# Key scale from raw keys, key splits inside the head steps, and the first score row through two banks

## The reference

```python
x = x + xattn(layernorm(x), ctx_512, ...)      # 16 heads over 4096 context rows of width 128
x = x + attn(layernorm(x), ...)                # 16 heads over the 256 tokens
x = x + ffn(layernorm(x), ...)                 # quantised weights and activations

# xattn, the part that this change touches
q_big = rope((hidden_q @ Wq.T per head) @ w_kc_q)        # 384 per head
kv_r  = rope(kv_c)                                       # 4096 x 128
scores = (q_big @ W_qr) . (kv_r @ W_kr)
attn  = softmax(scores)
ctx   = (attn @ kv_r) @ w_kc_kv
out   = ctx @ Wo.T
```

## Time and profile before

| | before |
|---|---|
| median of 3 runs | 576.0 us (575.85 to 577.02) |
| the profiled execution | 576.91 us, span 575.0 us |
| mean granted TensorE clock | 0.979 |
| TensorE, VectorE, ScalarE, GpSimd busy | 92%, 84%, 63%, 27% of the span |
| share of TensorE in the chain that ended last | 63% |

### The profile page before, as it was taken

One profiled execution on the slowest core, in us unless ns is written; L12 is line 12 of the kernel. 1 busy time (PEld: TensorE's weight loads), 2 busy tenths in 40 slices (PEclk: granted clock), 3 DMA queues, 4 the chain that ended last, 5 costly groups with the idle time before them and its releaser, 6 DMA issues.

```text
span 575.0 us, 9999 instructions
## 1 busy us (share of the span) xinstructions
PE 530.1 (92%) x3799; PEld 352.6 (61%) x3803; DVE 482.6 (84%) x716; ACT 363.4 (63%) x442; POOL 153.4 (27%) x186
## 2 busy tenths in 40 slices
PE   7999955789999999999999999999989998996896
PEld 3876722356666666666666666666667773454442
DVE  3588796899989999999999999999977366489986
ACT  1133460978788688687786886887885334896142
POOL 2359943101112202202102102201000001598401
PEclk9999996999999999999999999999998998999799
DMA  8998127599999999999999999999999989100001
GB/s 315 338 364 255 63 49 174 159 203 196 201 193 204 200 190 204 210 212 210 206 199 205 203 196 203 197 201 205 196 194 181 273 358 395 82 0 1 1 0 38
DMA packets 287806, 107.41 MB, mean 187 GB/s; under 512 B 276896, under 2 KB 277920, under 8 KB 286368
## 3 DMA queue, kind: packets, MB, share of 16 engines
q1 hardware_dynamic: 287776, 107.01, 85.6%
HBM read 37.26 MB, written 0.52 MB: 66 GB/s over the span
## 4 chain that ended last, share of the span: by engine, by line
PE 63%; DVE 18%; DMA 5%; issue 5%; ACT 4%; POOL 4%; SPq 0%; DVEq 0%; ACTq 0%
PE ps L646 16%; PE ps L648 8%; PE ps L628 8%; PE ps L630 8%; PE ps L629 8%; DMA pT<-split 4%; PE ps L748 4%; DVE rows L1233 3%; POOL qrope L480 2%; DVE split L1215 2%; DVE qrope L1265 2%; DVE qrot L1271 1%; DVE KL L1253 1%; PE ps L677 1%; PE ps L850 1%
## 5 line engine op out<-in xcount | busy, mean ns | idle before, releaser
L646 PE MATMUL ps<-pT,VH 128*128 128x256 f16 x1024 | 196.8, 274 | 1.9 <-DMA pT<-split 1.9
L648 PE MATMUL ps<-pT,VL 128*128 128x128 f16 x1024 | 183.4, 220 | 0.0
L1233 DVE TENSOR_SCALAR_CACHE_REDUCE rows<-ps,qback 128x1024 f32<-128x1024 f32 x128 | 163.6, 1280 | 17.5 <-PE ps L630 16.8
L1003 ACT ACTIVATE split<-rows,rz 128x2048 f16<-128x2048 f32 x64 | 124.8, 1995 | 67.5 <-DVE rz L1184 67.4
L1215 DVE SCALAR_TENSOR_TENSOR split<-rows,rz,split 128x2048 f16<-128x2048 f32 x64 | 150.3, 2350 | 1.3 <-issue 1.2
L989 ACT ACTIVATE rows<-rows,negm 128x2048 f32<-128x2048 f32 x64 | 127.2, 1988 | 0.2 <-DVE negm L1238 0.2
L646 PEld LDWEIGHTS ps<-pT,VH 128*128 128x128 f16 x1024 | 100.5, 98 | 42.8 <-DMA pT<-split 4.9
L648 PEld LDWEIGHTS ps<-pT,VL 128*128 128x128 f16 x1024 | 100.6, 98 | 27.3
L628 PE MATMUL ps<-KH,qcur 128*128 128x512 f16 x256 | 97.8, 382 | 14.0 <-DVE qcur L1290 10.7
L509 POOL TENSOR_TENSOR ctx_c<-acc 128x128 f32<-128x128 f32 x32 | 24.4, 762 | 296.8 <-ACT acc L978 296.8
L629 PE MATMUL ps<-KL,qcur 128*128 128x512 f16 x256 | 97.5, 381 | 0.0
(11 more groups left out here) (172 smaller groups left out, 656.1 us busy)
## 6 DMA issues: line engine op xcount, KB each, us to landing
w_sb<-w SPq DMA_DIRECT2D x3, 2816.0 KB, 15.8
wq_sb<-wq SPq DMA_DIRECT2D x4, 1024.0 KB, 8.6
wo_sb<-wo SPq DMA_DIRECT2D x16, 256.0 KB, 4.5
wkcq_sb<-wkcq SPq DMA_DIRECT2D x4, 768.0 KB, 9.3
keys<-ctxT SPq DMA_DIRECT2D x8, 256.0 KB, 7.7
stage<-ctxT SPq DMA_DIRECT2D x16, 128.0 KB, 8.0
stage<-kcos SPq DMA_DIRECT2D x8, 256.0 KB, 7.8
stage<-ksin SPq DMA_DIRECT2D x8, 256.0 KB, 9.3
```

Of the source, the lines that this page charges most:

```text
L646: nc.tensor.matmul(bank(6 + r % 2, 0, 256), VH[:, 4 * b + k, :], p.rearrange("p x q -> p (x q)"), start=(b == 0 and k == 0), stop=False)
L648: last = nc.tensor.matmul(bank(6 + r % 2, 0, 128), VL[:, 4 * b + k, :], p[:, 0, :], start=False, stop=(b == 7 and k == 3))
L1003: nc.scalar.activation(split[:, split_slot(r, half), :, 0, :], rows[:, k, half * 2048:(half + 1) * 2048].rearrange("p (b k) -> p b k", k=1 ...
L1233: nc.vector.tensor_scalar(rows[:, k, c * 1024:(c + 1) * 1024], ps[:, score_bank(s) * 512:(score_bank(s) + 2) * 512], qback[:, r // 2:r // ...
```

## The change

On SyncE, the raw load of a block of keys leaves `load_ctx` and becomes `load_raw`, with a semaphore of its own, and most raw loads are moved ahead of others. On ScalarE, the magnitude sums are taken of the raw keys, as soon as they are loaded, in place of the rotated ones. A rotated pair (a, b) mixes the two partitions 64 apart, so VectorE adds to each sum that of the other half (`kother`). The key scale is then made at p = 8 in place of 14; the products of the keys (GpSimd) come in other steps and wait for the magnitude sum of their block; KH and KL are made block by block in steps 9 to 13 and 10 to 14 in place of 15 to 17 and 16 to 18. The first query total moves from 16 to 10, the first query's halves from 18 to 15. Row 0's score steps come two by two at the end of steps 15 to 18, all through banks 0 and 1, with their copies in VectorE's steps 16 to 19; four steps of row 1 come at the start of steps 19 and 20. The key transposes wait for all rotated keys in place of all projections.

The sum of magnitudes before the rotation is not that after it, so the scale has another value than before; it is divided out again later.

```diff
-    EARLY = NCH
-    KEY_STEP = (0, 3, 5, 7, 8, 10, 11, 12)
-    HIGH_FIRST = (0, 3, 6, NCH)
-    LOW_FIRST = (0, 2, 4, NCH)
+    EARLY, EARLY_COPIED = NCH + 4, NCH + 2
+    RAW_STEP = (-1, 2, 4, 4, 5, 5, 6, 6)
+    KEY_STEP = (0, 2, 4, 6, 8, 9, 10, 11)
+    HIGH_STEP = (9, 9, 9, 10, 10, 11, 12, 13)
+    LOW_STEP = (10, 10, 10, 11, 11, 12, 13, 14)
...
+            def load_raw(n):
+                blk = slice(n * 512, (n + 1) * 512)
+                sp.dma_start(keys[:, blk], ctxT[:, blk]).then_inc(raw_in[n], 16)
...
             load_wq(0)
+            load_raw(0)
             load_ctx(0)
...
+            load_raw(1)
             load_ctx(1)
             load_wq(1)
+            load_raw(2)
+            load_raw(3)
             load_wqr(0)
...
+            load_raw(4)
+            load_raw(5)
+            load_ctx(2)
             load_wq(2)
-            load_ctx(2)
+            load_raw(6)
+            load_raw(7)
             load_wkcq(1)
             load_ctx(3)
...
-            sp.wait_ge(qhk_done, XH // 2)
+            sp.wait_ge(kr_done, NCH)
...
-                    pool.wait_ge(ctx_in[n % 4], 80 * (n // 4 + 1))
+                    pool.wait_ge(kabs_done, n + 1)
+                    pool.wait_ge(ctx_in[n % 4], 64 * (n // 4 + 1))
...
                     if j % 2 == 0:
-                        wait(pe, row_copied, 4 * row + j // 2 - 2)
-                    o = bank(score_bank(s) + j % 2)
+                        wait(pe, row_copied, j // 2 if first_row else 4 * row + j // 2 - 2)
+                    o = bank((0 if first_row else score_bank(s)) + j % 2)
...
+                if 19 <= p < 21:
+                    for s in range(2):
+                        attention_step(0, TURN - 8 + 2 * (p - 19) + s)
...
-                if p == 16:
+                if p == 10:
                     query_total(0)
-                if p >= 18:
-                    first = TURN - 16 + (0, 4, 6, 8)[p - 18]
-                    for s in range(first, TURN - 16 + (4, 6, 8, 8)[p - 18]):
-                        attention_step(0, s)
+                if 15 <= p < 19:
+                    for s in range(2):
+                        attention_step(0, TURN - 16 + 2 * (p - 15) + s)
...
+            def raw_sum(n):
+                act.wait_ge(raw_in[n], 16)
+                wait(act, kabs_done, n)
+                key = slice(n * 512, (n + 1) * 512)
+                nc.scalar.activation(absolute[:, :], keys[:, key], ACT.Abs, accum_out=kpart[:, n:n + 1]).then_inc(kabs_done, 1)
...
-                if 15 <= p < 18:
-                    for n in range(HIGH_FIRST[p - 15], HIGH_FIRST[p - 14]):
+                for n in range(NCH):
+                    if HIGH_STEP[n] == p:
                         key_high(n)
-                if p == 18:
+                if p == 15:
                     act.wait_ge(qhk_done, XH // 2)
...
+                for a, b in ((0, 64), (64, 0)):
+                    link(nc.vector.tensor_copy(kother[a:a + 64], ksum[b:b + 64]))
+                link(nc.vector.tensor_tensor(ksum[:, :], ksum[:, :], kother[:, :], ALU.add))
...
-                if p == 14:
+                if p == 8:
                     key_scale()
-                if p == 15:
+                if p == 9:
                     query_part(0)
-                if p == 17:
+                if p == 11:
                     query_factor(0)
...
-                if 16 <= p < 19:
-                    for n in range(LOW_FIRST[p - 16], LOW_FIRST[p - 15]):
+                for n in range(NCH):
+                    if LOW_STEP[n] == p:
                         key_low(n)
-                if p == 18:
+                if p == 15:
                     dve.wait_ge(qcur_first, 1)
...
+                if 16 <= p < 21:
+                    attention_step(0, 33 + 2 * (p - 16))
...
-            attention_step(0, 33)
-            attention_step(0, 35)
-            attention_step(0, 37)
-            attention_step(0, 39)
             query_part(1)
             query_factor(1)
-            attention_loop(dve, attention_step, EARLY, AVLAG)
+            attention_loop(dve, attention_step, EARLY_COPIED, AVLAG)
```

More of the change, by code:

```diff
@@ L164, in program @@
         ksum = small("ksum", [128, 1])
+        kother = small("kother", [128, 1])
         kinv = small("kinv", [128, 1])
@@ L298, in program @@
         ctx_in = [sem(f"ctx_in{k}") for k in range(4)]
+        raw_in = [sem(f"raw_in{k}") for k in range(NCH)]
         wo_in = [sem(f"wo_in{k}") for k in range(4)]
@@ L944, in _ @@
                     nc.scalar.activation(qrT[:, n // 2 % 2, :], bank(6, 0, TOK), ACT.Copy).then_inc(qr_copied, 1)
-                if p - 2 in KEY_STEP:
-                    n = KEY_STEP.index(p - 2)
-                    act.wait_ge(kr_done, n + 1)
-                    wait(act, kabs_done, n)
-                    key = slice(n * 512, (n + 1) * 512)
-                    nc.scalar.activation(absolute[:, :], keys[:, key], ACT.Abs, accum_out=kpart[:, n:n + 1])\
-                        .then_inc(kabs_done, 1)
-                if 15 <= p < 18:
-                    for n in range(HIGH_FIRST[p - 15], HIGH_FIRST[p - 14]):
+                for n in range(1, NCH):
+                    if RAW_STEP[n] == p:
+                        raw_sum(n)
+                for n in range(NCH):
+                    if HIGH_STEP[n] == p:
                         key_high(n)
-                if p == 18:
+                if p == 15:
                     act.wait_ge(qhk_done, XH // 2)
@@ L1231, in attention_step @@
                             dve.wait_ge(qbig_done, XH)
+                    o = 0 if isinstance(i, int) and row == 0 else score_bank(s)
                     nc.vector.tensor_scalar(rows[:, k, c * 1024:(c + 1) * 1024],
[L1234 removed]
+                                            ps[:, o * 512:(o + 2) * 512], qback[:, r // 2:r // 2 + 1], None,
                                             ALU.mult, ALU.max, accum_out=mx[:, k, c:c + 1]).then_inc(row_copied, 1)
```

10 lines of the change are left out of this document (4 added, 6 removed).

## The result

| | before | after |
|---|---|---|
| median | 575.9 us (575.84 to 577.02, 4 runs) | 595.0 us (592.98 to 595.96, 4 runs) |
| the profiled execution, its span | 576.91, 575.0 | 594.23, 592.0 |
| mean granted TensorE clock of it | 0.979 | 0.971 |
| end of the first query | 92.54 | 90.27 |
| first exponential | 103.23 | 119.66 |

A forecast was written before the change was run, and what follows sets the result against it. TensorE bounds the kernel (92% busy), so a shift of the first rows moves the end one for one. First query -4.4 and two-bank scores +14.2 give +9.8, taken as +9.0 on 576.0: 585.0 us, range 579.5 to 590.

The forecast's parts named there:

- the closed chain: Steps 16 and 17: scores, head product, signal, rotation and copy wait for each other in turn, 6.7 us each, 13.4 together.
- paper: Each engine's queue through the head laid out by hand in program order, with VectorE and GpSimd operations excluding each other.
- gain at the first query: End of the head: key splits taken out of TensorE's gap make the first query ready 4.4 us earlier.
- query to exponential, waits: First query to first exponential: row 0 through two banks takes 24.9 us against 10.7, 14.2 lost.
- deduction for the layout's lateness: First exponential: +9.8 taken as +9.0, because the old order's layout runs late where GpSimd and VectorE collide.
- rival (b): Steps 15 to 18: TensorE's clock falls to half, some 5 us of its work doubles: 590 us, chance 0.11.
- The layout of the old order: Hand-laid queues of the kernel before: first query at 94.2 (trace 92.54), first exponential at 104.7 (trace 103.23).
- the sum of loads: Head: raw blocks 3 to 7 ahead of the second key-query weights, which come 3.6 us later, at 35.8.
- (a): Steps 10 to 14: low halves hardly wait for GpSimd, 0.61 each, +4.9: 581 us, chance 0.15.
- (c): Head: VectorE keeps up, the gap is gone, TensorE's work hides the copies; 6 us faster, 570, chance 0.07.
- (d): Head: no collisions, query at 77.4, but the closed chain; exponential at 102.3, 575 us, chance 0.05.
- (e): Head: the change fails its purpose, for instance high halves wait for a late scale; slower still, chance 0.02.

The follow-up runs named there:

- experiment 6: The changed kernel with the second group of key-query weights loaded ahead of raw blocks 4 to 7: 593.4 us, ratio 1.029.
- experiment 1: The changed kernel with matmuls nobody reads put into TensorE's waits in the head, to keep its clock up: 589.3 us, ratio 1.022.
- experiment 3: The changed kernel with low halves subtracting a PSUM bank in place of KH (one SBUF input, result not the real one): 581.6 us, ratio 1.008.
- experiment 4: The changed kernel with row 0's scores put back to steps 18 to 20 and four banks, copies after the loop: 577.8 us, ratio 1.001.
- experiment 5: The kernel of experiment 4, but with row 0's scores through banks 0 and 1 alone: 581.9 us, ratio 1.007.
- experiment 9: The kernel of experiment 4 with key products earlier, low halves over steps 10 to 16 reading high halves from PSUM, first query in 16: 574.6 us, ratio 0.995.
- experiment 7: The kernel before the change with 39 matmuls nobody reads in its 10.67 us gap before row 0's first score: 576.1 us, ratio 0.996.
- experiments 9 and 11: The latter: the kernel of experiment 9 with matmuls nobody reads before the first query total and row 0's first score: 573.2 us, ratio 0.994.
- experiment 10: The changed kernel with VectorE's score copies ahead of rotations in steps 16 to 20, and unread matmuls in steps 10, 13, 15: 585.0 us, ratio 1.014.

## Why the prediction was wrong, step by step

**What held.** The direction; the closed chain, found before the run by reading two queues side by side, at 6.8 us a pair against 6.7; step 14 at 71.96 (paper 72.7); the first query at 90.27 (paper 89.8); the low halves at over 2 us beside GpSimd; the wait for weights in step 6 at 2.19, where 2 to 3 were forecast, harmless (experiment 6); the wait at the first total, 1.82 against 2.3; VectorE's steps 8 to 13, 35.3 us together against 36.2; the shift carried on nearly one for one.

**The sum at the first exponential: 9.0 forecast, 16.4 measured.** The 7.4 between them:

| step of the sum | forecast | measured | missed |
|---|---|---|---|
| gain at the first query | -4.4 | -2.3 | 2.1 |
| query to exponential, waits | +14.2 | +14.9 | 0.7 |
| query to exponential, clock | 0 | +3.8 | 3.8 |
| deduction for the layout's lateness | -0.8 | 0 | 0.8 |
| sum | +9.0 | +16.4 | 7.4 |

The measured 14.9 is 18.7 less 3.8 of experiment 1.

**The step that failed most** is the clock. It stood as rival (b) with 0.11, though its size was well found (some 5 us, measured 3.8 by this part and 5.7 by the medians). The argument against it was that the stretch that fell was busy for 3.40 of 8 us and that the new one would be busy for about half of its time. After had 5.67, 4.60 and 4.61 busy of 8 and lost the clock in all three windows, with gaps of 3.21, 3.90 and 3.40 us in front. The rows of before even had the hint: the clock fell some 3 us into the gap, and I had forecast gaps of about 3. The Trainium skill, page TensorE: Matmul & The Clock Gate, section HAM oscillation — how this bites in real kernels, describes a kernel whose waits between short bursts bring the clock down again at each; this trace agrees, with 3.4 us at half clock around the end of each of the waits of 3.21 and 3.40, and 6.9 around that of 3.90. It doesn't happen at each such wait: it did behind 1.82 us in step 10 of after, and not behind 2.59 there, nor behind 3.40 in experiment 3. It should have been a term of the sum with a range, not a rival. Even as the rival it was priced at 590, 5 short of the 595.0, because it stood on the same sum.

**The difference of two layouts.** The layout of the old order put the first query 1.7 late (94.2 against 92.54), that of the new one was not late at all (89.8 against 90.27). I subtracted one from the other, which kept the 1.7 as if it were a gain, and then took 0.8 off again in the belief that the new order would be later still on paper. The new layout's own 114.7 (89.8 and 24.9) less the trace's 103.23 would have given +11.5; with the clock's 3.8 that is 15.3 of the measured 16.4. Why the old layout was late is not settled. Which side of a collision goes first is one candidate: a low half that loses takes 2.40 in place of 0.75, and on paper the first to come always won. The prediction also misread one of its prices: the key addition of 0.69 at 52.16 was not made beside an idle GpSimd; GpSimd's sum began 0.05 us behind it and took 2.31 in place of 1.81.

**Two small terms.** The operations added for the key scale were to cost 0.5 us at most and took 1.7, from 49.77 to 51.49, of which the addition alone 1.31. And the loads of a block are 1024 KB together, not the 1280 that the prediction names; the sum of loads doesn't use that number, and TensorE's product with those weights began at 35.87, forecast 35.8.

**From the exponential to the median.** The span grew by 17.0, 0.6 more than the first exponential moved, and the time around it by 0.3 (594.23 less 592.0, against 576.91 less 575.0); the medians differ by 19.0, since before's profiled execution lay 1.0 above its median and after's 0.7 below. I had treated the first as an offset to take off. The 0.6 arose inside the cross attention; behind it both take 148.4 us (spans less these starts):

```profile
426.56 1.99 ACT L989 ACTIVATE rows<-rows,negm 128x2048 f32<-128x2048 f32 x1
```
```profile
443.61 1.99 ACT L1008 ACTIVATE rows<-rows,negm 128x2048 f32<-128x2048 f32 x1
```

Other executions of after had mean clocks of 0.968 to 0.983 and the fastest had the highest, so they likely lose the clock in other places; their timelines weren't recorded.

**The rivals.** (a) was wrong on the collisions, and its price was nearly right: with 0.61 for each low half it had +4.9 at the exponential, and experiment 3 has +6.2 there, of which 1.3 is the clock in its first pair (8.11 apart against 6.79); by medians it is 4.2 slower than before (0.6% to 1.1%). The collisions themselves were priced at 4.1 (9.0 less 4.9) and moved the first query by 7.7. (c) fell on both conditions: VectorE's steps 10 to 12 took 8.7, 8.3 and 5.4 us, and each pair of scores waited for its copy. (d), no collisions but the closed chain, is nearest to experiment 3: it had the query at 77.4 and the whole at 575, against 82.56 and 581.6. Experiment 3 cures only the low halves, though. Key additions of 2.28 and the small operations of 1.32 and 1.77 us were still in it, and no run of the new order is without them. (e) is excluded by the low halves, which began at 59.9 in place of 79.9.

**A claim that the result alone would not have shown wrong** is that the splits' place was itself a part of the loss. With row 0's scores put back (experiment 4) it costs nothing measurable. The costs don't add: undoing the clock, the order, the collisions or the scores takes off 5.7, 9.3, 13.4 and 17.2, 45.6 together from a loss of 19. In the stretch from query to exponential two of them can be laid side by side: 29.4 us in after, 25.6 with a full clock, 21.7 with the other order, 20.4 with both. That is 3.8 and 7.7 alone and 9.0 together: where the order took the waits away, little was left for the clock to lose.

## What to carry to other kernels

When work is put into the steps of a loop that is written out on several engines, read the queues of two engines side by side: if A's new work waits for B's, and B's stands behind something that waits for A, each step costs the whole round, whatever each engine's busy share is; try the other order on B first (here 9.3 us for a few moved lines). Turning one long gap into several of some 3 us was no gain for TensorE's clock here (3.8 us lost where it had been 1.4), and which of them bring it down was not to be foretold, so price the work behind them at full and at half clock, as bounds. Anchor a paper layout of a new order on its own absolute times as well as on the difference to a layout of the old one, and give the two as bounds. And before a position in one trace is compared with that in another, see where the two first part: several of these heads were 0.6 to 2.2 us late before any edit acted.

## What the runs showed of the hardware

- Which side wins a collision between VectorE and GpSimd can't be told from the recorded starts. In after VectorE's began 0.05 us ahead of GpSimd's twice; once VectorE took 0.75 and GpSimd 2.37, once 2.40 and 1.81. Kernels with the same code there had 0.75 and 0.75 (experiment 4) or 2.40 and 2.40 (experiment 5). The runs of such kernels also spread more: 574.6 to 580.8 in experiment 4, 573.9 to 575.8 in experiment 9, where no low half collides. But none collides in experiment 3 either, and eight of its nine runs spread over 580.0 to 584.4, so that the one causes the other is not shown.
- A small instruction can pay as much as a large one. In after the addition of two 128x1 columns took 1.31 us and the scaling of a 128x2 tile 1.77 us; each ended with a sum of GpSimd that had begun before it. Others of their size took 0.1 to 0.2 us. The same scaling took 0.23 in the kernel before, where it began 0.05 us ahead of the sum, and 1.88 in experiment 7, where it did too:

```profile
50.14 1.31 DVE L1211 TENSOR_TENSOR ksum<-ksum,kother 128x1 f32<-128x1 f32 x1
...
55.09 1.77 DVE L1221 TENSOR_SCALAR qtotal<-qpart,kinv 128x2 f32<-128x2 f32 x1
```

- Products that nobody reads kept the clock up wherever they ran in time: by medians 5.7 us in after and 1.9 in the kernel before (3.8 and 1.4 on the path from query to exponential), 1.5 between experiments 9 and 11 (0.7 by the ratios, within the noise), and nothing in experiment 10, where one of them itself waited.
